# One turning matmul a pair for both batches' low-rank columns, with the products of A00 and A01 moved ahead of it

## What is computed

```python
w = weights[conditions]                              # (64,128,128), picked per batch
x = x + einsum('bct,bcd->bdt', x, w)                 # batch b: (I + w)^T x, x is 128 x 1024
H   = einsum('btd,od->bto', x, W)                    # 1024 x 1024 dense layer
xa  = einsum('btd,brd->btr', x, A[adapter_idx])      # rank 16, one of 8 adapters per batch
x = x + H + einsum('btr,bor->bto', xa, B[adapter_idx]) * s[adapter_idx]
```

## Time and profile before

| | us |
|---|---|
| median of 3 runs | 771.11 (771.02 to 771.27) |
| the profiled execution, its own time | 771.08 |
| its span | 769.2 |
| PE busy / DVE busy / ACT busy / POOL busy | 761.3 / 612.7 / 504.3 / 196.8 |

### The profile page before, as it was taken

The page is one execution under the profiler, slowest core; times in us unless marked ns, Lnnn a source line. Parts: engine busy times, 40 slices in busy tenths (PEclk is TensorE's granted clock), DMA queues, the critical chain, the costliest instruction groups (busy, mean ns, idle before and its releaser), DMA issues.

```text
span 769.2 us, 16746 instructions
## 1 busy us (share of the span) xinstructions
PE 761.3 (99%) x4432; PEld 721.5 (94%) x4432; DVE 612.7 (80%) x1386; ACT 504.3 (66%) x1173; POOL 196.8 (26%) x428
## 2 busy tenths in 40 slices
PE   8999999999999999999999999999999999999998
PEld 5667999999999999999999999999999999999997
DVE  6899977879777788777888777888777888777774
ACT  3476666676666676666676666676666676666673
POOL 5633211332311333212333211333212233212200
PEclk9999999999999999999999999999999999999999
DMA  9333334442334342334442343442343432343222
GB/s 321 138 131 144 124 121 147 125 149 90 111 128 147 125 148 86 116 127 139 134 144 80 114 140 129 143 132 84 124 137 123 150 129 84 121 143 123 89 90 83
DMA packets 47291, 98.32 MB, mean 128 GB/s; under 512 B 6438, under 2 KB 25894, under 8 KB 47270
## 3 DMA queue, kind: packets, MB, share of 16 engines
q1 hardware_dynamic: 46832, 97.68, 37.6%
q10 hardware_dynamic: 438, 0.39, 0.2%
HBM read 63.45 MB, written 34.60 MB: 127 GB/s over the span
## 4 chain that ended last, share of the span: by engine, by line
PE 90%; DVE 2%; issue 0%; ACT 0%; DVEq 0%; ACTq 0%
PE bank L1394 75%; PE o_ps L1455 4%; PE bank L1433 4%; PE o_ps L1454 4%; PE o_ps L1456 4%; DVE c_sb L904 0%; DVE z_lo L901 0%; DVE x_lo L901 0%; PE o_ps L1445 0%; PE bank L1438 0%; DVE x_raw L901 0%; DVE w_lo L901 0%; ACT z_hi L518 0%; DVE bank L904 0%; PE bank L1454 0%
## 5 line engine op out<-in xcount | busy, mean ns | idle before, releaser
L1394 PE MATMUL bank<-w_hi,x_hi 128*128 128x342 f32 (+2 forms) x1200 | 390.4, 325 | 1.1 <-ACT c_sb L518 1.1
L1394 PE MATMUL bank<-w_lo,x_hi 128*128 128x342 f32 (+2 forms) x1200 | 387.1, 323 | 0.0
L1394 PE MATMUL bank<-w_hi,x_lo 128*128 128x342 f32 (+2 forms) x1200 | 386.5, 322 | 0.0
L1394 PEld LDWEIGHTS bank<-w_hi,x_hi 128*128 128x128 f32 x1200 | 225.8, 188 | 9.7 <-ACT c_sb L518 2.2
L1394 PEld LDWEIGHTS bank<-w_lo,x_hi 128*128 128x128 f32 x1200 | 225.6, 188 | 2.8
L1394 PEld LDWEIGHTS bank<-w_hi,x_lo 128*128 128x128 f32 x1200 | 226.1, 188 | 0.0
L901 DVE TENSOR_TENSOR x_lo<-x_raw,x_hi 128x256 fp32r<-128x256 f32 (+1 forms) x270 | 145.0, 545 | 31.3 <-ACT x_hi L518 26.7
L518 ACT ACTIVATE x_hi<-x_raw 128x256 fp32r<-128x256 f32 (+1 forms) x270 | 133.8, 507 | 53.9 <-PE bank L1394 45.7
L303 POOL TENSOR_TENSOR w_lo<-a_ride,w_hi 128x160 fp32r<-128x160 f32 x30 | 15.6, 521 | 503.5 <-ACT w_hi L518 503.5
L518 ACT ACTIVATE c_sb<-bank 128x342 f32<-128x342 f32 x190 | 85.7, 452 | 41.4 <-PE bank L1394 39.0
L518 ACT ACTIVATE z_hi<-c_sb 128x340 fp32r<-128x340 f32 (+1 forms) x128 | 60.3, 490 | 53.0 <-DVE c_sb L904 53.0
(11 more groups left out here) (106 smaller groups left out, 888.1 us busy)
## 6 DMA issues: line engine op xcount, KB each, us to landing
x_raw<-xT SPq DMA_DIRECT2D x62, 512.0 KB, 4.2
out<-o_sb SPq DMA_DIRECT2D x62, 512.0 KB, 2.6
b_stack_raw<-b_split SPq DMA_DIRECT2D x128, 128.0 KB, 2.5
...
```

What stands on the lines that cost most here:

```text
L1394: last = nc.tensor.matmul(bank[:, lo:hi], x[:, left, c * C:(c + 1) * C], w[:, c, FIRST[o]:FIRST[o] + WIDTH[o]], start=opens and c == 0 and ...
```

## The change

1. Both batches' columns go into one `xa_cols`, batch 0 in rows 0 to 63 and batch 1 in rows 64 to 127 of what comes out, and one `turn` a pair turns both, behind product "19". `turned_xa` copies the half that is its own; the other halves of the two `g_sb` are zero from the start. Pair 31 keeps two turns (`last_end`).
2. For this, products "1" and "3" (with A00 and A01; "3" completes batch 0's 16 columns) stand together ahead of the second half of `condition0`, and L11, L10, L12 and L00 stand behind product "6". Only L01 and L02 are left for the next pair's step.
3. The lists of ACT and DVE are written anew from pair 0's end on: for pairs 0 to 3 each by itself, for the loop, and for the last pair (`last_step`).
4. The block b32 is loaded into the place of product "8"'s high weights instead of "16"'s, so that DVE can make the sums "16a", "16", "19a" and "19" before it waits for product "17" of pair 1.

The diff, cut to its core ("..." marks what is left out):

```diff
-             "b11": ("lo", "6"), "b32": ("lo", "16"), "b31": ("lo", "12"), "b02": ("lo", "1"), "b10": ("lo", "3"),
+             "b11": ("lo", "6"), "b32": ("hi", "8"), "b31": ("lo", "12"), "b02": ("lo", "1"), "b10": ("lo", "3"),
...
-    SPLITS = ("17", "13", "5", "15", "2", "0", "4", "14", "18", "10", "7", "11", "9", "8", "16", "1", "3", "19", "6", "12")
+    SPLITS = ("17", "13", "5", "15", "2", "0", "4", "14", "18", "10", "7", "11", "9", "16", "8", "1", "6", "3", "19", "12")
+    RESTS = ("17", "13", "5", "15", "2", "0", "14", "18", "10", "4", "7", "11", "9", "8", "16", "19", "1", "12", "6", "3")
...
-                after(sp, lora_done["00"], i, j, d - 1)
+                after(sp, lora_done["02"], i, j, d - 1)
...
             def turned_xa(i, j, d, n):
-                after(act, turned[n], i, j, d)
-                if n:
-                    after(act, lora_done["12"], i, j, d - 1)
+
+                rows = slice(n * P // 2, (n + 1) * P // 2)
+                alone = n and not exists(i, j, 1)
+                if alone:
+                    act.wait_ge(turned_alone, 1)
                 else:
-                    after(act, lora_done["00"], i, j, d - 1)
-                copy(g_sb[n][:, :], o_ps[1][:, 0:P] if n else bank_of(j, d, "alpha")[:, H - P:H]).then_inc(g_ready[n], 1)
+                    after(act, turned, i, j, d)
+                after(act, lora_done["12" if n else "02"], i, j, d - 1)
+                copy(g_sb[n][rows, :], o_ps[1][rows, 0:P] if alone else bank_of(j, d, "alpha")[rows, H - P:H])\
+                    .then_inc(g_ready[n], 1)
...
+            i, j = 0, 1
+            copy_c17(i, j)
+            hi_z01(i, j, -1)
+            copy_c5(i, j)
             whole_block("02", c02_sb, "pi02")
-            copy_c5(0, 1)
-            hi_z02(0, 1, -1)
-            begin_c10(0, 1)
-            evacuate(0, 1, -1, 1, 0)
+            hi_z02(i, j, -1)
             made(act, "9", "f")
             in_place("9")
...
-            seed_pi11(0, 1)
-            in_place("8")
-            evacuate(0, 1, -1, 1, 1)
+            evacuate(i, j, -1, 1, 0)
+            begin_c10(i, j)
             made(act, "6", "16")
             in_place("16")
-            begin_c11(0, 1)
-            seed_pi10(0, 1)
-            hi_u(0, 1, 1)
-            hi_u12(0, 1, 1)
+            seed_pi11(i, j)
+            made(act, "9", "16a")
+            in_place("8")
...
+                split_xa0(i, j)
+                rest_u910(i, j, 1)
+                rest_xa0(i, j)
+                if exists(i, j, 2):
+                    sum_u12(i, j, 2)
+                rest_u11(i, j, 1)
+                rest_u3(i, j, 1)
+                half_c12(i, j)
+                rest_c(i, j)
+                sum_c11(i, j)
+                sum_c10(i, j)
+                sum_c12(i, j)
+                rest_a02(i, j, 1)
+                if exists(i, j, 2):
+                    begin_u(i, j, 2)
+
+            def last_step(i, j):
+                rest_z("11", i, j, -1)
...
+            made(dve, "i32")
+            add("16a", slot("lo", "16"), slot("lo", "8"), w_block("b32"), ALU.subtract)
             rest_z("10", 0, 0, 0)
             rest_z("11", 0, 0, 0)
-            dve.wait_ge(product_done["17"], 1)
-            add("9", w_block("b12"), w_block("b12"), w_block("b32"), ALU.subtract)
-            rest_z("12", 0, 0, 0)
-            rest_z("01", 0, 0, 0)
+            made(dve, "16a", "i22")
+            add("16", slot("lo", "16"), slot("lo", "16"), w_block("b22"), ALU.subtract)
             rest_z("00", 0, 0, 0)
-            made(dve, "9")
-            add("16a", w_block("b32"), slot("lo", "8"), w_block("b32"), ALU.subtract)
-            rest_z("02", 0, 0, 0)
-            made(dve, "16a", "i22")
-            add("16", w_block("b32"), w_block("b32"), w_block("b22"), ALU.subtract)
+            dense_through(dve, "b22")
             made(dve, "16")
             add("19a", w_block("b22"), w_block("b22"), slot("hi", "12"), ALU.subtract)
             made(dve, "19a")
             add("19", w_block("b22"), w_block("b22"), slot("hi", "6"), ALU.subtract)
+            rest_z("12", 0, 0, 0)
+            rest_z("01", 0, 0, 0)
+            dve.wait_ge(product_done["17"], 1)
+            add("9", w_block("b12"), w_block("b12"), w_block("b32"), ALU.subtract)
+            rest_z("02", 0, 0, 0)
+
+            i, j = 0, 1
             split_after("5", "5")
-            sum_u12(0, 1, 1)
...
-            def turn0(i, j):
+            def turn(i, j):
+
                 after(pe, xa_ready[0], i, j, 0)
-                nc.tensor.matmul(bank_of(j, 0, "alpha")[:, H - P:H], xa_cols[0][:, :].bitcast(f32r), ident_r[:, :],
-                                 start=False, stop=True, skip_group_check=True).then_inc(turned[0], 1)
-
-            def turn1(i, j):
+                after(pe, xa_ready[1], i, j, 0)
...
-            def loras0(i, j, d):
-                after(pe, g_ready[0], i, j, d)
+            def rest_loras0(i, j, d):
                 lora("01", i, j, d)
                 after(pe, c12_half, i, j, d)
                 lora("02", i, j, d)
-                lora("00", i, j, d)
 
...
+            def end(i, j):
                 left("u3", i, j)
                 multiply("16", "pi12", i, j).then_inc(product_done["16"], 1)
+                after(pe, c02_begun, i, j, 0)
+                left("a001", i, j)
+                multiply("1", "alpha", i, j)
+                multiply("3", "alpha", i, j).then_inc(product_done["3"], 1)
                 if exists(i, j, -1):
                     condition0(i, j, -1, 1)
+                left("a02", i, j)
+                after(pe, c_block["12"], i, j, -1)
+                multiply("19", "pi02", i, j, True).then_inc(product_done["19"], 1)
+                turn(i, j)
+                after(pe, c02_half, i, j, 0)
+                multiply("6", "beta", i, j).then_inc(product_done["6"], 1)
+                after(pe, g_ready[1], i, j, 0)
+                after(pe, b_ready, i, j, 0)
+                lora("11", i, j, 0)
+                lora("10", i, j, 0)
+                lora("12", i, j, 0)
+                after(pe, g_ready[0], i, j, 0)
+                lora("00", i, j, 0)
+                left("a03", i, j)
+                multiply("12", "beta", i, j).then_inc(product_done["12"], 1)
+
+            def last_end(i, j):
+
+                turn1_alone(i, j)
+                left("u3", i, j)
+                multiply("16", "pi12", i, j).then_inc(product_done["16"], 1)
+                condition0(i, j, -1, 1)
                 after(pe, c02_begun, i, j, 0)
```

More of the change, by code:

```diff
@@ L201, in cond_resid_kernel, with run_steps @@
         block = ctx.enter_context(nc.Block())
-        def run_steps(eng, step, first=1):
+        def run_steps(eng, step, last_step, first=1):
             with eng.Fori(first, NP // 2 - 1) as i:
@@ new lines, in step @@
+                hi_u11(i, j, 1)
+                hi_rides(i, j, 1)
+                hi_a02(i, j, 1)
+                turned_xa(i, j, 0, 1)
+                hi_of_c(i, j)
+                turned_xa(i, j, 0, 0)
+                hi_a001(i, j, 1)
+                hi_z00(i, j, 0)
+                evacuate(i, j, -1, 0, 1)
+                hi_z11(i, j, 0)
+                hi_z10(i, j, 0)
+            def last_step(i, j):
+                copy_c17(i, j)
+                hi_a03(i, j, 0)
+                hi_z12(i, j, -1)
+                copy_c5(i, j)
+                hi_z01(i, j, -1)
+                begin_c10(i, j)
+                evacuate(i, j, -1, 1, 0)
+                seed_pi11(i, j)
+                hi_z02(i, j, -1)
+                begin_c11(i, j)
+                hi_u54(i, j, 0)
+                evacuate(i, j, -1, 1, 1)
+                seed_pi10(i, j)
+                take_b(i, j)
+                begin_c12(i, j)
+                seed_pi12(i, j)
@@ L849, in _ @@
             copy_c17(i, j)
+            hi_z01(i, j, -1)
             hi_z12(i, j, -1)
-            hi_z00(i, j, -1)
+            copy_c5(i, j)
+            begin_c10(i, j)
+            seed_pi11(i, j)
+            hi_z02(i, j, -1)
+            evacuate(i, j, -1, 1, 0)
+            hi_u54(i, j, 0)
+            begin_c11(i, j)
+            hi_u12(i, j, 1)
+            seed_pi10(i, j)
+            seed_pi12(i, j)
+            evacuate(i, j, -1, 1, 1)
+            begin_c12(i, j)
+            hi_a13(i, j, 1)
+            hi_a1(i, j, 1)
+            hi_u(i, j, 1)
+            take_b(i, j)
+            begin_c02(i, j)
+            evacuate(i, j, -1, 0, 0)
+            hi_u67(i, j, 1)
+            hi_rides(i, j, 1)
+            hi_u3(i, j, 1)
+            hi_u910(i, j, 1)
+            turned_xa(i, j, 0, 1)
+            hi_u11(i, j, 1)
+            turned_xa(i, j, 0, 0)
+            hi_of_c(i, j)
+            evacuate(i, j, -1, 0, 1)
+            hi_a02(i, j, 1)
+            hi_z00(i, j, 0)
+            hi_z11(i, j, 0)
+            hi_z10(i, j, 0)
+            hi_a001(i, j, 1)
+            i, j = 1, 1
+            copy_c17(i, j)
+            hi_a03(i, j, 0)
+            hi_z12(i, j, -1)
```

(50 more changed lines are left out.)

410 lines of the change are left out of this document (226 added, 184 removed).

## The result

The changed kernel takes 777.54 us (median of 4 runs, 777.33 to 777.85) against 771.19 (771.02 to 771.45) for the kernel before in the same session: a ratio of 1.0082, with a 95% interval of 1.0065 to 1.010. It is slower by 6.4 us. The forecast of 766.4 has the wrong sign and the range of 765.0 to 769.8 doesn't hold the result. The profiled executions, 777.33 and 771.08, have spans of 775.56 and 769.23, which are 6.3 apart, so the spans show the whole difference.

The account below looks back on a forecast made before the run. The prediction took PE, busy 761.3 of 769.2 us, to bound the kernel. Its terms, -3.2 - 0.2 - 1.66 - 0.28 + 0.7 = -4.6, took 771.1 to 766.5, put at 766.4 us; range 765.0 to 769.8.

Parts of the forecast that it names:

- What bounds the kernel: Whole kernel: PE, busy 761.3 of 769.2 us, is the bound; gains are its work per pair and waits near the start.
- What a turn costs: PE, each pair: a turn costs 0.11 us, so one less in pairs 2 to 30 saves 3.2 us.
- Does the turn's answer come back in time?: ACT's copies of g to PE's low-rank matmuls: just in time or 0.02 us late; price taken as 0 a pair.
- T: Start time of the pair's new turn on PE, from which the prediction counts its times in us.
- The first rival: Hand-overs: g or `sum_c11` reaches PE 0.05 to 0.15 us late in every pair; 769.3 us in all; chance 0.17.
- Is the bank free for the next "17"?: DVE before product "17": `sum_c11` ends at T + 2.30, wanted by about T + 2.4; cost 0, thin cover.
- The slower rival: Product "17" waits for `sum_c11`, 0.3 us late in each of 29 pairs: 8.7 us more, 775.1; chance 0.10.
- The store and SP's queue: SP: batch 0's store waits for an `evacuate` at the pair's end, loads behind it wanted 8 us later or more; cost 0.
- Start: Pairs 1 to 3: 1.66 us won back in pair 2 and 0.28 in pair 3, 0.7 lost in pair 1.
- Pair 2 at 23.3: Pair 2's predicted length in us, down from 25.10, chiefly by ending PE's 1.06 us wait for `begin_c10`.
- Pair 3's 0.28: Pair 3: its 0.28 us of waits beyond pair 14's length would be won back.
- `begin_c10` in pair 1: ACT's copy ahead of product "2", standing behind the in-place high part of "9": cost 0.7 us, bounds 0 and 1.2.

Follow-up runs that it names:

- full-height runs: Changed kernel with `turned_xa` copying all 128 rows instead of its batch's 64: for both batches 769.35 us, for batch 1 only 769.40 us.

## Why the prediction was wrong, step by step

- **What bounds the kernel** was right: a pair of the loop takes what PE's work takes and what makes PE wait, and nothing else.
- **What a turn costs**, 0.11: right. 23.16 against 23.06 gives 0.10, and 27 such pairs are 2.7 us. The saving was there all the time, under the loss. The two gaps that the Trainium skill has (TensorE: Matmul & The Clock Gate, "Back-to-back issue gap"), 56 and 81 ns, are both below it.
- **Does the turn's answer come back in time?** This is the step that failed. "Batch 1's g starts at T + 0.57 and ends at T + 0.85" was T + 0.70 and T + 0.97 (T = 367.48); "batch 0's g at T + 1.06, ending at T + 1.34" was T + 1.44 and T + 1.71. All of the error is in one rule taken over from other rows: "ACT starts its next instruction some 0.10 before the last one ends". That was read off two copies that both start at partition 0. The change brought the first copies that don't. The line "half the partitions make a copy no shorter, I assume" asked how long such a copy takes and not what it does to its neighbours. The first rival had the right place and waits, and allowed 0.05 to 0.15 a pair for it; they were 0.34. The full-height runs and the run with the copies side by side show this on the chip.
- **Is the bank free for the next "17"?** The bound of T + 2.30 with 0.1 to spare was somewhat too good: in the full-height run `sum_c11` ends at T + 2.45. With the hand-over mended, 0.03 to 0.08 a pair was lost here, 1.1 to 1.3 us in all by the loop's periods. In the changed kernel itself this cost nothing, since its "17" came 0.34 later. The slower rival, 0.3 a pair here, did not occur: that the whole came out slower, as it said, was luck, since the loss came from another mechanism.
- **The store and SP's queue**: cost 0 for the store held. The loads did cost: `take_b` in pair 1 waited 1.08 for b. The step said that the loads behind the store are wanted "8 us later or more"; the new list of pair 1 wants b about 3.5 us earlier than the old one (48.71, where it was 52.20).
- **Start.** Pair 2 at 23.3 was right to 0.01. Pair 3's 0.28 didn't come; `sum_c01` is late there behind `rest_u67`. `begin_c10` in pair 1 cost 0.24 where 0.7 was taken, inside its bounds of 0 and 1.2, and `seed_pi10` behind `take_b` cost 0.88, which wasn't in the sum: no step asked what the early copy of b holds up on ACT. The start's two stalls of pair 1 make 1.12 for the 0.7.

Put together, with a turn's 0.11 in the pairs it belongs to, predicted and measured: pair 2 begins at +0.5 and +1.03; pair 2 takes -1.77 and -1.77; pair 3 -0.39 and +0.26; pairs 4 to 30 -3.0 (27 x 0.11) and +6.7; the end 0 and +0.1. The sums are -4.7 and +6.3. Of the difference of 11.0, the loop has 9.7: 27 x 0.34 = 9.2 for the hand-over of g, and 0.3 for a turn of 0.10 in place of 0.11; the rest is rounding. The start has 0.5 + 0.65, and the end 0.1, whose cause I didn't trace.
